# Layer 0 attention: the contexts of an even and an odd group of heads share one block of 128 rows

## The reference, cut to what matters

```
q = proj(wq, bq); k = proj(wk, bk); v = proj(wv, bv)      # 16 heads of 16
scores = einsum('bhqd,bhkd->bhqk', q, k) / sqrt(16)
attn = softmax(scores)
ctx = einsum('bhqk,bhkd->bhqd', attn, v)
ctx = ctx.transpose(0, 2, 1, 3).reshape(B, S, D)          # 4 x 512 x 256
return ctx @ wo.T + bo
```

## Time and profile before

| | us |
|---|---|
| three runs | 1424.57, 1425.9, 1441.39 |
| median | 1425.9 |
| the profiled execution: its own time | 1425.93 |
| span of its trace, first to last instruction | 1424.6 |
| attention of layer 0 in it | 0 to about 334 |
| granted TensorE clock, mean over the span | 0.950 of full |

### The profile page before, as it was taken

How to read it: one execution, slowest core, us unless ns; L and a number is a source line. 1 busy time by engine, 2 the same in 40 slices (tenths; PEclk the granted TensorE clock), 3 DMA queues, 4 the chain that set the end, 5 groups by cost and what they waited for, 6 DMA issues and landing times.

```text
span 1424.6 us, 22581 instructions
## 1 busy us (share of the span) xinstructions
PE 1280.9 (90%) x6461; PEld 906.7 (64%) x6461; DVE 870.1 (61%) x2637; ACT 783.5 (55%) x1919; POOL 457.3 (32%) x589
## 2 busy tenths in 40 slices
PE   6589998887799998799999999999999977999994
PEld 5334443335456776577777777787877754677773
DVE  5668887754652365665577567756676755433555
ACT  3268675663432445676667666665666643166552
POOL 5344644220435644200010025001500150455553
PEclk9679999997999999899999999999999997999997
DMA  7732616215113553044100001000100019455764
GB/s 218 143 79 56 120 49 138 78 35 217 58 41 115 158 155 103 33 149 153 56 1 1 16 8 53 1 16 1 53 9 16 1 57 365 163 154 154 209 200 132
DMA packets 79207, 133.99 MB, mean 94 GB/s; under 512 B 13788, under 2 KB 52708, under 8 KB 77420
## 3 DMA queue, kind: packets, MB, share of 16 engines
q1 hardware_dynamic: 62128, 92.39, 20.7%
q0 software_dynamic: 15712, 38.25, 10.0%
q10 hardware_dynamic: 1248, 1.90, 0.4%
HBM read 77.20 MB, written 60.00 MB: 96 GB/s over the span
## 4 chain that ended last, share of the span: by engine, by line
PE 66%; DVE 14%; issue 7%; ACT 5%; DMA 5%; POOL 4%; SPq 0%; DVEq 0%; ACTq 0%; POOLq 0%
PE psum L126 8%; PE psum L128 7%; PE psum L127 7%; PE psum L2008 7%; PE psum L2658 7%; PE psum L2704 5%; PE psum L2531 4%; PE psum L1979 3%; PE psum L854 3%; PE psum L883 3%; PE psum L2565 2%; DVE psum L1943 2%; DVE a_nmax L790 2%; PE psum L2627 1%; PE psum L778 1%
## 5 line engine op out<-in xcount | busy, mean ns | idle before, releaser
L790 DVE TENSOR_REDUCE a_nmax<-psum 128x2 f32<-128x1024 f32 x128 | 154.9, 1215 | 56.6 <-PE psum L778 55.5
L1954 ACT ACTIVATE a_spare<-psum,a_nmax 128x128 f32<-128x128 f32 (+3 forms) x256 | 134.7, 526 | 90.9 <-DVE a_nmax L1943 82.2
L869 ACT ACTIVATE a_et<-psum 128x512 f32<-128x512 f32 x256 | 139.0, 594 | 81.2 <-PE psum L854 77.5
L2727 POOL DMA_INDIRECT results<-r_fin,r_to x134 | 134.3, 1002 | 123.5 <-ACT r_fin L2719 60.6
L2008 PE MATMUL psum<-a_et,a_v 128*128 128x512 f32 (+3 forms) x512 | 169.9, 434 | 1.8 <-DVE a_ctx L2025 1.6
L1943 DVE CUSTOM_DVE_ANT_0 psum<-psum,a_spare 128x128 f32<-128x128 f32 (+3 forms) x256 | 127.1, 496 | 63.0 <-PE psum L128 56.5
L2658 PE MATMUL psum<-m_w,m_xT 128*128 x536 | 150.4, 403 | 0.0
L1988 ACT ACTIVATE a_et<-psum 128x128 f32<-128x128 f32 (+3 forms) x256 | 111.4, 435 | 44.6 <-PE psum L1979 42.0
L126 PE MATMUL psum<-a_kT,a_q 128*128 128x128 f32 (+3 forms) x256 | 118.8, 464 | 6.6 <-DVE a_q L1882 5.9
L854 PE MATMUL psum<-a_stk 50*128 50x512 f32 x256 | 105.8, 480 | 18.4 <-ACT a_et L869 12.3
L1979 PE MATMUL psum<-ident,a_spare 128*128 128x128 f32 x640 | 113.2, 275 | 1.0 <-DVE a_spare L1967 1.0
(11 more groups left out here) (329 smaller groups left out, 3007.8 us busy)
## 6 DMA issues: line engine op xcount, KB each, us to landing
r_xs<-slots SPq DMA_DIRECT2D x134, 129.0 KB, 2.3
slots<-empty SPq DMA_DIRECT2D x12, 1290.0 KB, 6.0
m_w<-in_experts SPq DMA_DIRECT2D x16, 768.0 KB, 14.3
stacks<-a_qk SPq DMA_DIRECT2D x32, 256.0 KB, 3.7
a_stk<-stacks POOLq DMA_DIRECT2D x32, 256.0 KB, 5.1
r_shared_hid<-results SPq DMA_DIRECT2D x12, 512.0 KB, 4.8
m_w<-in_experts SPq DMA_DIRECT2D x4, 1216.0 KB, 14.2
a_stk<-stacks POOLq DMA_DIRECT2D x32, 128.0 KB, 5.7
```

Of the source, the lines that this page charges most:

```text
L790: dve.tensor_reduce(nmax[:, G % 2, qt, 2 * p:2 * p + 2], psum[:, n:n + 2, :], AX.X, ALU.max, negate=True).then_inc(s_max.sem, 1)
L869: act.activation(et[:, n % NET, 2 * p + hh, :], psum[:, 4 + hh, :], ACT.Exp).then_inc(s_e.sem, 1)
L1954: act.activation(e[:, u % NE, 0:W], psum[:, n, 0:W], ACT.Exp, bias=nmax[:, u % NE, :], scale=-1.0, accum_out=rsum[:, u % NE, :]).then_inc( ...
L2727: pool.indirect_dma_start(results[:, :], bass.IndirectOffsetOnAxis(ap=to[:, i % NI, 0:1].bitcast(U32), axis=0), ys[:, o, :], None, bounds_ ...
```

## The change

The context of an even group is no longer kept in a block of its own. After the normalisation, the 16 context rows of each head of the even group and those of the odd group behind it are written side by side, to two halves of 32 rows in one tile `both`. One transpose, one rounding and one subtraction then serve the two groups, in the steps of the odd one. The weight `w0_o` is laid out without zero rows as two blocks of 128 rows. The projection contracts two blocks instead of four. The steps of the last batch's pieces become `((40, 41), (52, 52))`.

```
-        wo_hi, wo_lo = sb("wo_hi", [P, GROUP0 * D], F32R), sb("wo_lo", [P, GROUP0 * D], F32R)
+        wo_hi, wo_lo = sb("wo_hi", [P, PAIRS0 * D], F32R), sb("wo_lo", [P, PAIRS0 * D], F32R)
+        both = sb("both", [P, S])[:, :]
-        staged += [(ins["w0_o"], wo_hi, wo_lo, c) for c in range(GROUP0 * D // S)]
+        staged += [(ins["w0_o"], wo_hi, wo_lo, c) for c in range(PAIRS0 * D // S)]
...
+        halves = both.rearrange("p (c g i) -> p g c i", g=2, i=HD0)
         def vector_sums(G):
             if G:
-                dve.wait_ge(*ctx_done[G - 1])
+                dve.wait_ge(*ctxn_done[G - 1])
             dve.wait_ge(*pv_done[TT * G + TT - 1])
             dve.transpose(cT, psum[:, 6, :]).then_inc(s_cT.sem, 1)
...
         def gpsimd_normalise(G):
             pool.wait_ge(*rinv_done[G])
-            pool.tensor_tensor(blocks[:, :, 0:HD0], blocks[:, :, 0:HD0],
+            if G % 2 == 0 and G:
+                pool.wait_ge(*ctx_done[G - 1])
+            pool.tensor_tensor(halves[:, G % 2], blocks[:, :, 0:HD0],
                                rinv[:, :, :].broadcast_to([P, TT * 4, HD0]), ALU.mult).then_inc(s_ctxn.sem, 1)
...
         def vector_ctx(G):
-            if G:
-                dve.wait_ge(*ctx_ready[G - 1])
+            if G > 1:
+                dve.wait_ge(*ctx_ready[G - 2])
+            dve.wait_ge(*ctxn_done[G - 1])
             dve.wait_ge(*ctxn_done[G])
-            dve.transpose(ctx32, cT).then_inc(s_ctx.sem, 1)
+            dve.transpose(ctx32, both).then_inc(s_ctx.sem, 1)
...
         def tensor_out(b, m):
...
-            for gr in range(GROUP0):
-                c = slice(gr * D + m * P, gr * D + (m + 1) * P)
-                mm = k.mm3(psum[:, n, :], (wo_hi[:, c], wo_lo[:, c]), (ctx[:, 0, gr, :], ctx[:, 1, gr, :]), gr == 0,
-                           gr == GROUP0 - 1)
+            for two in range(PAIRS0):
+                c = slice(two * D + m * P, two * D + (m + 1) * P)
+                mm = k.mm3(psum[:, n, :], (wo_hi[:, c], wo_lo[:, c]), (ctx[:, 0, two, :], ctx[:, 1, two, :]), two == 0,
+                           two == PAIRS0 - 1)
...
-        def tensor_last_out(gr, m):
+        def tensor_last_out(two, m):
...
-            pe.wait_ge(*ctx_ready[GROUP0 * b + gr])
+            pe.wait_ge(*ctx_ready[GROUP0 * b + 2 * two + 1])
...
-        LAST_OUT, LAST_BACK_AT = ((36, 37), (40, 41), (47, 47), (52, 52)), 54
+        LAST_OUT, LAST_BACK_AT = ((40, 41), (52, 52)), 54
...
             for G, r in groups(s, CTX_AT + 2):
-                vector_ctx(G)
+                if G % 2:
+                    vector_ctx(G)
...
             for G, r in groups(s, CTX_AT + 3):
-                scalar_ctx(G)
+                if G % 2:
+                    scalar_ctx(G)
...
-                if G < NG - 1:
+                if G % 2 and G < NG - 1:
                     gpsimd_ctx(G)
...
-    wo_rows = np.zeros((H0, 32, D), np.float32)
-    wo_rows[:, :HD0] = wo.T.reshape(H0, HD0, D)
+    by_pairs = lambda w: w.reshape(PAIRS0, 2, GROUP0, HD0, -1).transpose(0, 2, 1, 3, 4).reshape(D, -1)
+    bv_rows, wo_rows = by_pairs(a["L0_attn_bv"]), by_pairs(wo.T)
```

More of the change, by code:

```diff
@@ L27 @@
 GROUP0 = 4
+PAIRS0 = H0 // GROUP0 // 2
 HALF0 = H0 // 4
@@ L517, in attention0 @@
         cT, ctx32 = turn_work[:, 0, :], turn_work[:, 1, :]
-        ctx = sb("ctx", [P, 2, GROUP0, S], F32R)
+        both = sb("both", [P, S])[:, :]
+        ctx = sb("ctx", [P, 2, PAIRS0, S], F32R)
         oT = sb("oT", [P, KT, S])
@@ L619, in tensor_bias @@
             pe.wait_ge(*small)
-            for j in (n_w, n_w + 1):
-                pe.wait_ge(*stage_in[j])
+            pe.wait_ge(*stage_in[n_w])
             if g.free[bank]:
@@ L624, in tensor_bias @@
             for m in range(KT):
-                for gr in range(GROUP0):
-                    c = (gr % 2) * D + m * P
-                    mm = pe.matmul(psum[:, bank, m:m + 1], stage(n_w + gr // 2)[:, c:c + P], bvp[:, gr:gr + 1],
-                                   start=(gr == 0), stop=(gr == GROUP0 - 1))
+                for two in range(PAIRS0):
+                    c = two * D + m * P
+                    mm = pe.matmul(psum[:, bank, m:m + 1], stage(n_w)[:, c:c + P], bvp[:, two:two + 1],
+                                   start=(two == 0), stop=(two == PAIRS0 - 1))
             mm.then_inc(s_o.sem, 1)
@@ L902, in vector_sums @@
             dve.wait_ge(*cT_done[G])
-            if G:
-                dve.wait_ge(*ctxn_done[G - 1])
             dve.reciprocal(rinv[:, :, :], blocks[:, :, HD0:HD0 + 1]).then_inc(s_rinv.sem, 1)
@@ L916, in vector_normalise @@
             dve.wait_ge(*rinv_done[G])
-            dve.tensor_tensor(blocks[:, :, 0:HD0], blocks[:, :, 0:HD0],
+            dve.tensor_tensor(halves[:, G % 2], blocks[:, :, 0:HD0],
                               rinv[:, :, :].broadcast_to([P, TT * 4, HD0]), ALU.mult).then_inc(s.sem, 1)
@@ L1159, in tensor @@
                     tensor_back(b, BACK_AT.index(d))
-                for gr in range(GROUP0):
+                for two in range(PAIRS0):
                     for m in range(KT):
-                        if b == B - 1 and d == LAST_OUT[gr][m]:
-                            tensor_last_out(gr, m)
+                        if b == B - 1 and d == LAST_OUT[two][m]:
+                            tensor_last_out(two, m)
                 if b == B - 1 and d == LAST_BACK_AT:
@@ L3139, in lay_out @@
         "w0_qkv": k_tiles(w0), "b0_qk": b0, "b0_v": bv_rows.reshape(-1, P).T,
-        "w0_o": k_tiles(wo_rows.reshape(-1, D)), "b0_o": a["L0_attn_bo"].reshape(KT, P).T,
+        "w0_o": k_tiles(wo_rows), "b0_o": a["L0_attn_bo"].reshape(KT, P).T,
         "rope": rope_table(), "ones": np.ones((2, 3 * HALF0 * S), np.float32), "mask": causal_mask(),
```

35 lines of the change are left out of this document (16 added, 19 removed).

## The result

The changed kernel takes 1420.9 us (median of 20 executions, 1412.8 to 1433.9), the kernel before 1431.1 us over 20 (1417.8 to 1442.9). The ratio is 0.9945 with a 95% interval of 0.9922 to 0.9967, so the gain is 7.9 us, and between 4.7 and 11.2. The forecast gain was 10.8 us, which this interval still takes in. The median of before was 1425.9 us when only three executions were known; the 20 put it 5.2 us higher (2.6 us without those three), and that is a large part of the 5.8 us by which the forecast time of 1415.1 is missed.

What follows compares the result with a forecast made beforehand. PE was taken to set the pace, with DVE close behind. Bursts 8.1 us plus last batch's pieces 2.7, all else 0, gave 10.8 us off 1425.9, so 1415.1 us; own range 1413 to 1417, widened to 1408 to 1424.

Steps and rivals of the forecast that it cites:

- rival 3: Behind each batch's projection: shortened bursts let the clock fall three times, net 3.5 us of loss, 1429.4 us; chance 0.05.
- The pieces of the last batch: Last batch: removed pieces at d = 36 and 37 save 2.7 us, the one at d = 47 is hidden, nothing.
- The bursts: Projection of batches 0 to 2: six bursts go from 12 to 6 matmuls, saving 8.1 us, bounds 4.2 and 8.4.
- rival 1: Behind the bursts: DVE and bank 7 take over half of their gain, leaving 6.9 us, 1419.0 us; chance 0.17.
- The contexts: Even groups' transposes, roundings and subtractions beside PE's matmuls: removing them saves nothing, at most 1 us.
- the new waits: POOL's multiplication of an even group now waits for the preceding odd group's transpose, six steps ahead: costs nothing.
- the start: At the start, one piece of `w0_o` less to load and split: saves 0, bounds 0 and 1.3 us.
- Rival 2: Last batch: without the removed pieces the clock may stay at half, leaving 8.7 us of gain, 1417.2 us; chance 0.20.
- one of the prediction's own signs of being wrong: Signs: DVE takes up the bursts' difference, clock at half longer in 300 to 325 us, or a later stage changes length.
- Rivals 4 and 5: Start gives 1.3 us and contexts 1, 1412.8 us, chance 0.13; full-row projection matmuls no cheaper, at most 1 us gain, 0.02.
- the second term: Last batch: the removed pieces at d = 36 and 37 save 2.7 us, bounds 0 and 2.7.

Runs made afterwards that it cites:

- e1: The kernel before, with two blocks instead of four contracted in each projection burst of batches 0 to 2: 1424.4 against 1437.2 us, ratio 0.9929.
- e3: The kernel before, without the last batch's pieces of its even groups (12 and 14): ratio 1.0016.
- e4: The changed kernel, with the last batch's removed matmuls put back at d = 36, 37 and 47 as filler into an unread bank: ratio 0.9970.
- g4: The changed kernel, with each product of batch 0's two bursts made twice, so 12 matmuls a burst there: ratio 0.9959.
- f3: The kernel before, without the even groups' transpose, rounding and subtraction, the projection reading odd groups' contexts in their place: ratio 1.0010.
- g3: The changed kernel, with a second output weight piece staged and split at the start and the bias product made over both pieces: ratio 0.9938.
- g2: The kernel before, with six filler matmuls ahead of the turned scores of groups 7 and 11: ratio 0.9974.
- f0: The changed kernel run again without any edit, on the chip of later runs: ratio 0.9957 against the kernel before.
- f1: The changed kernel, with six filler matmuls ahead of the turned scores of groups 7 and 11: 1419.0 us, ratio 0.9928.
- g1: The changed kernel, with six filler matmuls ahead of the turned scores of groups 7 and 11 and 24 before the last pieces: ratio 0.9937.

## Why the prediction was right or wrong

Three terms of the forecast were off. The sum had nothing for the clock behind the shortened bursts, where between the two profiles 3.1 us are given back at one place (rival 3 below). The pieces of the last batch were sized at 2.7 us and measured 1.5 to 2.1. And the base of 1425.9 us, which came from three executions, is 5.2 us below the median of 20; the profiled execution that agreed with it had a mean clock of 0.950, while the mean of before in the three later lots is 0.942 to 0.943, and 0.01 of clock is 9 to 10 us there. The interval of the whole gain (4.7 to 11.2 us) alone could not tell 7.9 from 10.8.

**The bursts: right.** 8.1 us were forecast, from the distance of 0.233 us between starts and not from the mean row of 469 ns. The pieces that hold the bursts are 2.83, 2.78 and 2.80 us shorter, 8.4 in all, and e1 gives 7.5 us at equal clock. DVE and bank 7 took nothing: rival 1 is out for the bursts themselves, since each piece became shorter by the full 2.8 us.

**The pieces of the last batch: too large.** 2.7 us were forecast, with bounds of 0 and 2.7. The term measured 1.5 us by taking them away (e3) and 2.1 by putting them back (e4). I had priced them by rows at half clock and in mid-change, 1.58 and 1.11 us, from one execution, and whether the clock is at half there differs from one to the next: in g4 the clock is back at 1.00 from 298 to 314 us, in the same stretch of its program. At full clock a piece adds 0.90 us to the chain (314.80 to 315.70 above; the first of three matmuls costs more than 0.233), so two such pieces are 1.8, which lies between the two measurements. That is the row to take when the clock of the place isn't the kernel's property but the execution's. That the piece at d = 47 was hidden held.

**The contexts, the new waits and the start: nothing that can be told, as forecast** (f3, and g3 for the start). In the waits of the changed kernel's trace the new ties cost 0.2 us in all, one wait of DVE's transpose (L928) for POOL's product (L912), which is off PE's path.

**Rival 2, the clock in the last batch.** The profile after looks like it: half clock from 302 us to the end, which is one of the prediction's own signs of being wrong (another, later stages of another length, came too: 2.1 us shorter, unexplained). But over all profiled executions turn 15 to the end takes 33.4 to 37.0 us with the old pieces or their fillers in place (before, e1, e4, f3, g2) and 32.6 to 40.4 without them. The profile after alone would have confirmed a mechanism that the others don't show.

**Rival 3, shortened bursts let the clock fall: dismissed for a wrong reason.** The prediction said that "the idle time of PE around them does not grow", and looked just behind the bursts. The fall comes 14 to 16 steps later, at PE's wait for the small rows of group 7: 0.93 to 1.55 us long with long bursts and 1.68 to 2.68 with short ones, with the clock falling each time in the second case alone. It costs 18.35 - 15.27 = 3.1 us between the two profiles, about what batch 0's shortened bursts save; g4, which undoes both, has a mean within 0.4 us of g3's. It isn't repeated in every batch as the rival had it, and it doesn't make the kernel slower.

**Rivals 4 and 5** are out: no start or context term shows, and the matmuls with full weight rows stand 0.233 us apart as before.

**The sum.** At equal clock the change is worth 9.1 us (f0) or 9.8 (g3), close to 7.5 for the bursts and 1.5 to 2.1 for the pieces. Against the forecast 10.8 this is 1 to 1.7 us less, for which the second term is enough within the uncertainty; but an equal clock also takes out what the fall at group 7 costs. As measured, 6.7 us in the mean of f0 and 8.3 of g3, the rest goes with a mean clock that is 0.0027 and 0.0015 lower than before's. The fall at group 7 fits this: some 7 us at half are 7 x 0.5 / 1417 = 0.0025 of the mean clock. But e1 has the same fall and a mean clock 0.0040 above before's, so this part is argued and not shown.

**Left open.** Why the small rows land later with short bursts: POOL issues them 2.96 us after turn 7 in every case, and the stack loads ahead of them in the queue 9.0 to 9.1 us before it; what differs is that the writes of the next batch's q and k stand 19.1 us ahead of the turn in place of 21.9. I didn't separate these. PE comes to the wait 5.9 us after turn 7 before and after the change; the rows are there 6.8 to 7.4 us after it with long bursts and 7.5 to 8.5 with short ones. And whether preventing the fall is worth anything for the whole kernel: f1 and g1 remove it, but the control g2 gained as much without having had it. All three kernels with fillers at the waits have a mean clock 0.004 to 0.005 above the same kernel without them (f1 over f0, g1 over g3, g2 over before), and means 2.0 to 3.1 us lower. The comparison at equal clock can't show such a gain, and e1 stands 0.004 above before without any filler, so it is neither shown nor ruled out. No version here is shown to beat the changed kernel.

## What to carry to other kernels

When work is cut from the engine that sets the pace, price it by the distance between starts at full clock (a run of three by its own rows, 0.90 us here and not 3 x 0.233), and look for the next wait of that engine on something that didn't become faster, also far downstream: the wait can grow there, as it did here some 25 us later, and the clock can fall behind it. Before a difference under 1% is explained from two profiles, plot the time of all executions against their mean granted clock; here 0.01 of clock is 9 us, more than the whole change. A control for a filler is the same filler in the kernel that doesn't need it.

## What the runs showed of the hardware

The mean granted clock of one and the same kernel differs from execution to execution (0.930 to 0.952 for the kernel before in one lot), and the half-clock stretches sit in different places each time: in the attention after 54 us 54 to 62, 70 to 88, 244 to 250, 302 to 310 and from 326 us on in the profile of before, 56 to 86, 234 to 242, 296 to 314 and 330 to 334 in that of f3, whose PE work up to there is the same. One place is different: behind group 7's wait the clock fell in six of six kernels with short bursts and no filler, and in none of six with long ones, one of which has fillers. A fall that holds for some 7 us, with a wait that is 0.44 us longer ahead of it, costs 3.1 us there.
